# A conditioned transformer layer: own output projection of the last sequence and first MLP weights inside its beats, an fp32 conditioning product, a table of its own for the first sequence

## The chip, the cores and the metric

The kernel runs on one core of one Trainium2 chip. The metric is the device time of one execution in microseconds, as the median of three runs. Below, PE is TensorE, ACT ScalarE, DVE VectorE, POOL GpSimd, and SP the engine that issues the DMA transfers.

## The reference

Everything is float32. There are 8 sequences of 512 tokens of width 512 (`x`) and one conditioning row of width 512 for each.

```python
cond = jax.nn.silu(c) @ wc.T + bc                        # 8 x 3072
sh1, sc1, g1, sh2, sc2, g2 = jnp.split(cond, 6, axis=-1)
h = _ln(x) * (1.0 + sc1) + sh1
x = x + g1 * _gqa_attn(h, wq, wk, wv, wo)                # 16 query heads, 4 key heads, head width 32
h = _ln(x) * (1.0 + sc2) + sh2
x = x + g2 * _mlp(h, w1, b1, w2, b2)                     # width 2048, exact gelu
```

`_gqa_attn` projects q, k and v, takes softmax(q k / sqrt(32)) v by head, and projects with `wo`.

## The kernel before

**Precision.** Large products run on operands split into a high and a low part of a faster float type. ACT copies the high part out of the accumulator bank, DVE subtracts it to get the low part, and PE makes three passes: high x high, high x low, low x high. Values (`values`) and softmax sums (`sums`) run in plain fp32; in them four products of 32 output rows each stand in four column groups of the array.

**The front** (`before` of each engine) is one order written out by hand, `FRONT`, that all engines follow, each doing its own part of a token. `Wc0.1` transposes piece 1 of the conditioning weights c0 (PE) and splits it (ACT `weight_high` L779, DVE `weight_low` L960); `Wk`, `Wq`, `Wv`, `Wo` do so for the projection weights. `Mc0.1` multiplies the piece with silu(c), both halves (`multiply`, L1206). `B0` adds the bias, `C0` turns the part into columns, `S` is silu. `X0` and `X1` are statistics and epsilon of sequences 0 and 1, `N0`, `N1` their norms, `T0` to `T3` the transposes of the normed x with modulation (L692) and split. `K`, `Q0` to `Q3`, `V` are projections; a letter a to d is a quarter, that is one tile of the contraction in three passes. `r0` to `r15` are the row products of group 0 (L1137) with their row maxima (L898), `s0` to `s4` the first of group 1, `t` turns the maxima. SP loads the raw weights and x, and moves K, Q and the maxima into the stacked tiles `k_stack` and `q_stack` (`stack_k`, `stack_q`, `stack_max`).

**A sequence** is 4 groups (one for each key head) of 16 beats. In every beat PE computes one score product (L1150), ACT its exp (L741), and PE one row product for a later group. In a group POOL adds the exps of the four key tiles (L607), PE forms values of two tiles in beat 5 and two in beat 11, and the sums in beat 5; then ACT and DVE invert, refine, divide and split. Between these, PE does the *fill* of the beat: a table gives for each beat the quarters of projections and the transposes. `FILL` serves sequences 0 to 6 (in sequence 0 without the O tokens), `LAST_FILL` sequence 7. `O0` to `O3` are the output projection of the sequence before; `VT` turns V. ACT takes a bank one beat after its token, DVE two or three.

**The last sequence** makes only two of the three adds of a group before the sums, and the sums of two tiles instead (8 products, L1173). Its own output projection, 4 tiles of 12 passes (L1082), comes after its last beat (`after`): groups 0 to 2 of tiles 0 and 1, weights 0 of the MLP turned, tiles 2 and 3, weights 1 turned, then group 3 of all tiles. Group 3 waits for the end of the softmax chain. `gate` (L948) takes each tile.

**The MLP** runs by sequence over 16 slices j: an up product of 12 passes (L1613), gelu and split, a down product of 12 passes into four banks (L1625). In its first sequence the weights of slice j + 1 are loaded through a ring of three, turned (L1379, L1384) and split just ahead. `WEIGHTS_AHEAD` says how many slices are turned before the loop.

The order that all this follows is the order of each engine's own instructions; semaphores join them. An engine that waits holds up everything behind it in its own order.

## Time and profile before

| | |
|---|---|
| Median of 3 runs | 1463.69 us (1463.34 to 1464.05) |
| Profiled execution | 1462.65 us, span 1460.9 us |
| PE busy | 1433.4 us, 98% |
| DVE, ACT, POOL busy | 708.7, 708.2, 569.4 us |
| Mean granted PE clock | 0.995 of full |
| HBM read, written | 55.44, 16.81 MB |

The profiled execution is one run. Its span goes from the first to the last instruction. Times of stages are cut from it: the front ends with the first score at 70.7 us, sequence 0 with the first score of sequence 1 at 146.6, sequence 7 has its last score at 717.3, and the second up product of the MLP starts at 737.8. Busy times of PE include the modelled ends of matmuls, which overlap the next ones; the distance between two starts is what one costs.

### The profile page before, as it was taken

The numbers are of one execution on the slowest core, as the hardware profiler recorded it, in microseconds if no ns is written. First come the engines' busy times: TensorE is split into PE (matmuls) and PEld (weight loads), VectorE is DVE, ScalarE is ACT, GpSimd is POOL, SyncE is SP. The second block draws the span as 40 slices with busy tenths as digits, with TensorE's granted clock in tenths as the row PEclk, the third lists the DMA queues.
The fourth block names the chain that finished last, engine by engine and source line by source line (L and its number), as shares of the span: only waits on it lengthen the run. The fifth ranks groups of instructions, "written<-read, shape, count | busy, mean of one in ns | idle before, by whom it ended". The sixth has DMA issues, their size and how long they took to land.

```text
span 1460.9 us, 19071 instructions
## 1 busy us (share of the span) xinstructions
PE 1433.4 (98%) x7021; PEld 1042.0 (71%) x7021; DVE 708.7 (49%) x1205; ACT 708.2 (48%) x1274; POOL 569.4 (39%) x230
## 2 busy tenths in 40 slices
PE   7899999999999999999999999999999999999998
PEld 5655666656656665665588888888888888888887
DVE  6877777776867787677534321222212122131212
ACT  6376758575666758575644423333233332323321
POOL 2067587676868687675310210121201212012210
PEclk9999999999999999999999999999999999999999
DMA  8232322324232322322352210201102020020100
GB/s 301 67 83 56 107 59 83 104 84 116 78 105 55 106 82 82 112 85 59 124 151 80 72 66 1 93 0 52 41 0 93 0 70 23 0 93 0 65 1 29
DMA packets 68435, 105.15 MB, mean 72 GB/s; under 512 B 10552, under 2 KB 19784, under 8 KB 68368
## 3 DMA queue, kind: packets, MB, share of 16 engines
q1 hardware_dynamic: 68368, 104.27, 23.2%
q8 instruction: 40, 0.66, 0.2%
q14 instruction: 27, 0.22, 0.1%
HBM read 55.44 MB, written 16.81 MB: 49 GB/s over the span
## 4 chain that ended last, share of the span: by engine, by line
PE 90%; DVE 5%; ACT 1%; POOL 1%; issue 1%; DMA 1%; SPq 1%; DVEq 0%; ACTq 0%; POOLq 0%
PE up L1613 24%; PE acc L1625 24%; PE proj_bank L1082 14%; PE key_bank L1150 8%; PE pv_bank L1159 7%; PE row_bank L1137 7%; DVE neg_max L898 3%; PE sum_bank L1173 2%; POOL probs_sum L607 1%; PE turn L1599 1%; PE proj_bank L1092 1%; SPq L486 1%; PE key_bank L1193 0%; ACT probs L741 0%; PE turn L1379 0%
## 5 line engine op out<-in xcount | busy, mean ns | idle before, releaser
L898 DVE TENSOR_REDUCE neg_max<-row_bank 128x1 f32<-128x512 f32 x512 | 337.4, 684 | 141.0 <-PE row_bank L1137 136.7
L741 ACT ACTIVATE probs<-key_bank 128x512 f32<-128x512 f32 x512 | 299.8, 598 | 163.2 <-PE key_bank L1150 159.8
L1613 PE MATMUL up<-h,w_t 128*128 128x512 f32 x1536 | 369.9, 390 | 0.0
L1625 PE MATMUL acc<-w_t,hidden 128*128 128x512 f32 x1536 | 369.6, 390 | 0.0
L1625 PEld LDWEIGHTS acc<-w_t,hidden 128*128 128x128 f32 x1536 | 287.9, 188 | 59.3
L1613 PEld LDWEIGHTS up<-h,w_t 128*128 128x128 f32 x1536 | 286.9, 188 | 58.5
L1544 DVE TENSOR_TENSOR hidden<-up,hidden 128x512 fp32r<-128x512 f32 x128 | 88.5, 692 | 482.6 <-ACT hidden L1495 482.6
L1486 ACT ACTIVATE up<-up,bias_cols 128x512 f32<-128x512 f32 x128 | 84.8, 662 | 421.9 <-PE up L1613 421.9
L607 POOL TENSOR_TENSOR probs_sum<-probs_sum,probs 128x2048 f32<-128x2048 f32 x59 | 271.8, 4607 | 14.4 <-ACT probs L741 7.9
L1150 PE MATMUL key_bank<-q_stack,k_stack 128*128 128x512 f32 x512 | 217.8, 429 | 2.6 <-ACT probs L741 2.5
L1137 PE MATMUL row_bank<-k_stack,q_stack 96*128 96x512 f32 x512 | 204.4, 410 | 4.2 <-DVE neg_max L898 3.6
L1457 POOL TENSOR_TENSOR y<-y,resid 128x512 f32<-128x512 f32 x30 | 37.8, 1293 | 365.1 <-DVE y L1553 365.1
L607 POOL TENSOR_TENSOR probs_sum<-probs 128x2048 f32<-128x2048 f32 x31 | 142.4, 4595 | 90.2 <-ACT probs L741 90.2
L1150 PEld LDWEIGHTS key_bank<-q_stack,k_stack 128*128 128x128 f32 x512 | 96.4, 189 | 83.5 <-issue 49.2
L1137 PEld LDWEIGHTS row_bank<-k_stack,q_stack 96*128 96x128 f32 x512 | 96.7, 189 | 39.8 <-DVE neg_max L898 17.0
L1159 PE MATMUL pv_bank<-probs,v 128*32 128x512 f32 x1024 | 123.1, 598 | 0.0
L1082 PE MATMUL proj_bank<-h,wq_t 128*128 128x512 f32 x384 | 110.4, 401 | 0.0
L1082 PE MATMUL proj_bank<-wo_t,attn 128*128 128x512 f32 x336 | 94.0, 394 | 0.0
L1434 POOL TENSOR_TENSOR rstd<-var_eps,neg_half 128x4 f32<-128x4 f32 x7 | 7.1, 1018 | 213.2 <-DVE var_eps L1530 213.2
L1082 PEld LDWEIGHTS proj_bank<-h,wq_t 128*128 128x128 f32 x384 | 72.3, 190 | 21.0 <-issue 5.9
L1495 ACT ACTIVATE hidden<-up 128x512 fp32r<-128x512 f32 x128 | 76.7, 599 | 11.6
L614 POOL TENSOR_TENSOR resid<-resid,gated 128x512 f32<-128x512 f32 x32 | 40.7, 1286 | 99.0 <-DMA resid<-in_x_dram 69.1
(155 smaller groups left out, 1129.4 us busy)
## 6 DMA issues: line engine op xcount, KB each, us to landing
q_stack<-spare SPq DMA_DIRECT2D x384, 64.0 KB, 2.0
xa<-in_x_dram SPq DMA_DIRECT2D x8, 1024.0 KB, 9.6
resid<-in_x_dram SPq DMA_DIRECT2D x8, 1024.0 KB, 7.0
x_scratch<-resid SPq DMA_DIRECT2D x8, 1024.0 KB, 4.5
xa<-x_scratch SPq DMA_DIRECT2D x8, 1024.0 KB, 5.7
spare<-in_L_cond_w_dram SPq DMA_DIRECT2D x32, 256.0 KB, 3.0
resid<-x_scratch SPq DMA_DIRECT2D x8, 1024.0 KB, 6.6
out_dram<-y SPq DMA_DIRECT2D x7, 1024.0 KB, 4.2
```

The costliest lines, as they stand in the source:

```text
L607: nc.gpsimd.tensor_tensor(probs_sum[:, :, :], first_in[:, :, :], probs[kt][:, :, :], ALU.add).then_inc(added, 1)
L741: nc.scalar.activation(probs[kt][:, r, :], key_bank[r % 2][:, :], ACT.Exp).then_inc(exp_done, 1)
L898: nc.vector.tensor_reduce(out=neg_max[:, g % 2, i:i + 1], in_=row_bank[(g + i) % 2][:, :], op=ALU.max, axis=AX.X, negate=True).then_inc(ro ...
L1082: last = nc.tensor.matmul(bank, lhs(i, kt), rhs(j, kt), start=(kt == 0 and (i, j) == (0, 0)), stop=(kt == KD - 1 and (i, j) == (1, 0)))
L1137: nc.tensor.matmul(row_bank[(g + i) % 2][:, :], q_stack[0:STACK, g, r, qt * P:qt * P + P], k_stack[0:STACK, g, :], start=True, stop=True). ...
L1150: nc.tensor.matmul(key_bank[r % 2][:, :], k_stack[:, g, kt * P:kt * P + P], q_stack[:, g, r, :], start=True, stop=True).then_inc(keys_scor ...
L1159: last = nc.tensor.matmul(pv_bank[HD * r:HD * r + HD, :], v[:, kt, g * HD:g * HD + HD], probs[kt][:, r, :], start=(kt == 0), stop=(kt == T ...
L1486: nc.scalar.activation(up[j % 2][:, :], up[j % 2][:, :], ACT.Gelu, bias=bias_cols[:, j:j + 1]).then_inc(gelu_done, 1)
L1495: nc.scalar.activation(hidden[j % 2][0][:, :], up[j % 2][:, :], ACT.Copy).then_inc(hid_hi, 1)
L1544: nc.vector.tensor_tensor(hidden[j % 2][1][:, :], up[j % 2][:, :], as_f32(hidden[j % 2][0][:, :]), ALU.subtract).then_inc(hid_split, 1)
L1613: last = nc.tensor.matmul(up[j % 2][:, :], w1_t[i][:, kt, j * P:j * P + P], h[k][:, kt, :], start=(kt == 0 and n == 0), stop=(kt == KD - 1 ...
L1625: last = nc.tensor.matmul(acc[tt][:, :], hidden[j % 2][i][:, tt * P:tt * P + P], w2_t[k][:, j, :], start=(j == 0 and n == 0), stop=(j == N ...
```

## The change

1. **Conditioning.** The conditioning weights are no longer split. ACT copies them as fp32 (`copy_weight`) into plain tiles, and PE multiplies two pieces at a time, one into output rows 0 to 7 and one into rows 32 to 39 of a bank; DVE adds both to the bias as before. c0 is loaded in two halves. The loads have a new order, given in `LOADS`, with `wq` ahead of x.
2. **The front's order** is new. `X1` and `N1` leave it; statistics and norms of sequence 1 stand in beats 0 to 11 of sequence 0.
3. **Sequence 0** gets its own fill table, `FIRST_FILL`.
4. **The last sequence** makes all three adds (the third on DVE in the last group, on POOL in the others) and sums of one tile. `U0`, `D0` to `U2`, `D2` turn and split the up and down weights of the first three MLP slices inside its beats, and the loads of these are issued after the maxima of group 2. `L0` to `L3` are quarters a and b (groups 0 and 1) of its own output projection. They use the row banks and the projection banks.
5. **After the last beat**: values, sums, quarter c of the four tiles, the first up product, then quarter d of the four tiles.
6. The MLP weights stand in one tensor `w_t`, by slice; the up banks now lie where the key banks were.

```diff
-WEIGHTS_AHEAD = 2
+WEIGHTS_AHEAD = 3
...
+FIRST_FILL = {
+    (0, 0): ("", "VT Q3a", "", "Q3b"),
+    (0, 1): ("Q3cd", "", "", ""),
+    (0, 2): ("", "", "", ""),
+    (0, 3): ("", "T0", "T1", ""),
+    (1, 0): ("", "", "T2", "T3"),
+    (1, 1): ("", "", "Kab", "Kc"),
+    (1, 2): ("Kd", "Q0ab", "", ""),
+    (1, 3): ("", "Q0c", "", "Q0d"),
+    (2, 0): ("", "", "", "Q1a"),
+    (2, 1): ("", "", "Q1b", ""),
+    (2, 2): ("", "Q1cd", "", "Q2a"),
+    (2, 3): ("Q2b", "", "Q2c", "Q2d"),
+    (3, 0): ("", "Va", "", "Vb"),
+    (3, 1): ("", "", "", ""),
+    (3, 2): ("", "Vcd", "", ""),
+    (3, 3): ("", "", "", ""),
+}
...
-    (0, 0): ("Q3a", "Q3bc", "", "Q3d"),
-    (0, 1): ("", "", "VT", ""),
-    (0, 2): ("", "", "", ""),
-    (0, 3): ("", "", "T0", ""),
-    (1, 0): ("O0a", "O0b", "", "O0c"),
-    (1, 1): ("", "", "O0d", ""),
-    (1, 2): ("", "O1ab", "", ""),
-    (1, 3): ("O1c", "", "", ""),
-    (2, 0): ("", "O1d", "O2a", ""),
-    (2, 1): ("", "", "O2b", ""),
-    (2, 2): ("O2c", "O2d", "", ""),
-    (2, 3): ("", "O3a", "", "O3b"),
-    (3, 0): ("", "O3cd", "", "T1 T2"),
-    (3, 1): ("", "", "", ""),
-    (3, 2): ("T3", "", "", ""),
-    (3, 3): ("", "", "", ""),
+    (0, 0): ("Q3a", "Q3b", "", "Q3cd"),
+    (0, 1): ("", "", "", ""),
+    (0, 2): ("VT", "", "", ""),
+    (0, 3): ("", "T0", "", ""),
+    (1, 0): ("O0ab", "", "", ""),
+    (1, 1): ("", "", "O0c", "O0d"),
+    (1, 2): ("O1a", "", "O1bc", ""),
+    (1, 3): ("O1d", "O2a", "", "O2b"),
+    (2, 0): ("O2c", "O2d", "U0", ""),
+    (2, 1): ("", "", "D0", ""),
+    (2, 2): ("", "T1", "", ""),
+    (2, 3): ("", "O3ab", "", "O3c"),
+    (3, 0): ("O3d", "U1", "T2 L0a", "L0b"),
+    (3, 1): ("D1", "", "", ""),
+    (3, 2): ("U2", "T3", "", "D2"),
+    (3, 3): ("L1a", "L1b", "", "L3ab L2ab"),
...
+FIRST_STATS = (0, 1, 2, 3)
+FIRST_MOMENTS = 4
+FIRST_EPS = 5
+FIRST_SHIFT = 7
+FIRST_NORM = (7, 9, 10, 11)
...
+    table = FIRST_FILL if not has_last else FILL if has_next else LAST_FILL
...
-S Wc0.0 Wc0.1 Wc0.2 Mc0.0 Wc0.3 Wc1.0 Wc1.1 Mc0.1 Mc0.2 Mc0.3 B0 X0 Wk.0 Wc1.2 C0 Mc1.0 Wc1.3 Mc1.1 Wq.0 Wq.3 Mc1.2
-Mc1.3 B1 N0 Wq.1 Wq.2 C1 Wc2.0 Wc2.1 Wv.0 T0 Mc2.0 Wc2.2 Wo.1 T1 Mc2.1 T2 Wc2.3 Mc2.2 Wc3.0 T3 Wo.2 Wo.0 Ka Mc2.3 B2 Kb
-Kc Kd Q0a Q0b Q0c Q0d Wc3.1 Mc3.0 Wc3.2 Wc3.3 Wo.3 Mc3.1 Mc3.2 Mc3.3 B3 r0 r1 Wc4.0 Q1a r2 r3 Wc4.1 Mc4.0 r4 C3 r5 Wc4.2
-Q1b r6 Wc4.3 Q1c r7 r8 Wc5.0 Mc4.1 Mc4.2 Mc4.3 r9 r10 B4 Q1d Va Wc5.1 Mc5.0 r11 r12 Vb r13 Mc5.1 r14 C4 r15 Wc5.2 b1
-Wc5.3 Vc t s0 Vd Mc5.2 X1 Q2a Mc5.3 s1 Q2b Q2c B5 s2 Q2d N1 s3 s4
+Wc0.0 Wc0.1 S Mc0.1 Wc0.2 Wc0.3 Mc0.3 Wc1.0 Wc1.1 Wc1.2 B0 X0 Mc1.1 Wc1.3 Wk.0 Wq.1 Wq.3 Wq.0 Mc1.3 B1 N0 C0 Wq.2 Wc2.0
+C1 Wc2.1 T0 Wo.1 Wc2.2 Wc2.3 T1 Mc2.1 Wo.2 T2 Wv.0 Mc2.3 T3 Wc3.0 Ka Kb Kc B2 Kd Q0a Wc3.1 Wc3.2 Q0b Wo.0 Q0c Q0d Wc3.3
+Wo.3 Mc3.1 Mc3.3 Q1a B3 r0 r1 Wc4.0 Wc4.1 C3 r2 Wc4.2 Q1b r3 r4 Mc4.1 r5 Wc4.3 r6 Wc5.0 r7 Q1c r8 Mc4.3 r9 r10 B4 Q1d Va
+r11 r12 Vb Wc5.1 Wc5.2 C4 Wc5.3 r13 Vc r14 Vd b1 r15 Mc5.1 t s0 Mc5.3 s1 Q2a s2 Q2b B5 s3 Q2c s4 Q2d
 """.split()
 FRONT += [f"s{i}" for i in range(5, 16)]
-RAW, EARLY = 4, 22
+RAW = 4
+LOADS = ('c1', 'q', 'x', 'k', 'c2', 'o', 'v', 'c4', 'c3', 'c5', 'b3', 'b4', 'b1')
...
+EARLY = sum(t[0] == "W" for t in FRONT[:FRONT.index("r0")])
...
+        w_t = sb(st, "w_t", [P, NJ, 4, N], f32r)
...
-            sums = [(g * GROUP + (kt + 1) * R, "sum", kt) for kt in range(1, adds_in(B - 1) + 1)]
+            sums = [(g * GROUP + (kt + 1) * R, "sum", kt) for kt in range(1, TT)]
...
-            return None if tt < 2 else row_bank[tt - 2]
+            return row_bank[tt] if tt < 2 else proj_bank[tt - 2]
...
+            def load_first_part():
+                for i in range(2):
+                    cols = slice(i * D // 2, i * D // 2 + D // 2)
+                    sp.dma_start(raw["c0"][:, :, cols], wc[0:D, cols].rearrange("(o p) i -> p o i", p=P)).then_inc(first_loaded[i], 16)
...
-                sp.dma_start(b1_rows[:, :], b1.rearrange("(j p) -> j p", p=P)).then_inc(b1_loaded, 16)
+                load_first_part()
+                for i in (0, 1, 2, 5):
+                    load_bias(i)
+                for name in LOADS:
+                    if name == "x":
+                        load_x(x, 0)
+                    elif name == "b1":
+                        sp.dma_start(b1_rows[:, :], b1.rearrange("(j p) -> j p", p=P)).then_inc(b1_loaded, 16)
+                    elif name in ("b3", "b4"):
+                        i = int(name[1])
+                        sp.wait_ge(cols_turned, i - 2)
+                        load_bias(i)
+                    elif name[0] == "c":
+                        if name == "c5":
+                            sp.wait_ge(w_turned, w_of("Wc1.3") + 1)
+                        load_part(int(name[1]))
+                    else:
+                        if name == "o":
+                            sp.wait_ge(w_turned, w_of("Wc0.3") + 1)
+                        load_raw(name, {"k": wk, "v": wv, "q": wq, "o": wo}[name])
...
-            def after(b):
+            def load_first_weights(b):
 
                 for g in range(HKV):
                     sp.wait_ge(k_stacked[g], b * STACKED + STACKED)
                     for i in range(2):
                         sp.wait_ge(q_stacked[i][g], queries_stacked(b, 2))
-                load_resid(b)
                 for j in range(RING):
                     load_weights(sp, j)
+
+            def after(b):
+                load_resid(b)
 
...
+            def first_high(name, u):
+                act.wait_ge(proj_ready, u.ready(name))
+                if name[1] != "0":
+                    act.wait_ge(proj_ready, u.ready("O3"))
+                nc.scalar.activation(first_weights(name, 0), proj_bank[u.bank(name)][:, :], ACT.Copy).then_inc(first_hi, 1)
...
-                if g == HKV - 1 and not has_next and 0 < kt <= adds_in(b) and r == R - 1:
+                if g == HKV - 1 and not has_next and kt > 0 and r == R - 1:
...
+            def turn_first(name, u):
+                j, half = int(name[1]), "UD".index(name[0])
+                bank = room(u, name)
+                pe.wait_ge(w_loaded[j], 32)
...
+            def own_part(tt, groups):
+
+                if 0 in groups and tt < 2:
+                    pe.wait_ge(row_taken, row_no(B - 1, HKV - 1, ROWS) + 1)
+                elif 0 in groups:
+                    for who in ("act", "dve"):
+                        pe.wait_ge(proj_taken[who], after_units().base[who])
+                out_part(B - 1, tt, None, groups, after_bank(tt))
+
             def out_part(b, tt, u, groups, bank=None):
 
                 if 0 in groups and bank is None:
                     room(u, f"O{tt}")
-                if tt == 0 or HKV - 1 in groups:
-                    pe.wait_ge(attn_split, b * HKV + (max(groups) + 1))
+                pe.wait_ge(attn_split, b * HKV + (max(groups) + 1))
...
-                pe.wait_ge(added, adds_no(b, g) + adds_in(b))
+                pe.wait_ge(added, adds_no(b, g) + (TT - 1))
                 if not is_first:
                     pe.wait_ge(attn_split, group_no(b, g))
-                summed = [probs_sum] + ([probs[TT - 1]] if adds_in(b) < TT - 1 else [])
-                if len(summed) > 1:
-                    pe.wait_ge(exp_done, exps_no(b, g, TT - 1) + R)
-                for i, tile in enumerate(summed):
-                    for r in range(R):
-                        last = nc.tensor.matmul(sum_bank[HD * r:HD * r + HD, :], ones[:, :], tile[:, r, :],
-                                                start=(i == 0), stop=(i == len(summed) - 1))
+                for r in range(R):
+                    last = nc.tensor.matmul(sum_bank[HD * r:HD * r + HD, :], ones[:, :], probs_sum[:, r, :], start=True, stop=True)
                 last.then_inc(sums_ready, 1)
...
+                n = products.index(w_of("W" + token[1:])) // 2
+                i, half = divmod(n, KD // 2)
+                pe.wait_ge(w_copied, 2 * n + 2)
                 if n == 0:
-                    pe.wait_ge(silu_split, 1)
-                if kt == 0 and i > 0:
+                    pe.wait_ge(silu_taken, 1)
+                if half == 0 and i > 0:
                     pe.wait_ge(part_biased, i)
-                for half in range(2):
-                    last = nc.tensor.matmul(cond_bank[0:SILU, :], silu_both[:, kt, :], wc_t[n % 3][half],
-                                            start=(kt == 0 and half == 0), stop=(kt == KD - 1 and half == 1))
+                for row, kt in ((0, 2 * half), (ODD_ROW, 2 * half + 1)):
+                    last = nc.tensor.matmul(cond_bank[row:row + B, :], silu_cols[:, kt, :], cond_tile(i * KD + kt),
+                                            start=(half == 0), stop=(half == 1))
                 last.then_inc(multiplied, 1)
...
-                    if tt == 2:
-                        pe.wait_ge(row_taken, row_no(b, HKV - 1, ROWS) + 1)
-                    out_part(b, tt, u, range(HKV - 1), after_bank(tt))
-                    if tt % 2 == 1:
-                        turn_weights(pe, tt // 2)
+                    own_part(tt, range(len(own_out(tt)), HKV - 1))
+                pe.wait_ge(proj_taken["dve"], u.base["dve"])
+                first_up(pe)
                 for tt in range(TT):
-                    out_part(b, tt, u, range(HKV - 1, HKV), after_bank(tt))
+                    own_part(tt, range(HKV - 1, HKV))
 
...
+        def up_product(pe, b, j, is_first):
+            if is_first and j < WEIGHTS_AHEAD:
+                pe.wait_ge(*first_split_done(j))
+            elif is_first:
+                pe.wait_ge(w_split, 2 * (j - WEIGHTS_AHEAD) + 2)
+            if not (is_first and j < 2):
+                pe.wait_ge(hid_split, b * NJ + (j - 1))
...
-                    up_product(b, j, is_first)
+                    if not (is_first and j == 0):
+                        up_product(pe, b, j, is_first)
```

## Rows read from the trace of the kernel before

**Rows 1.** The page, section 4: chain that ended last, shares by engine and line.

```profile
PE 90%; DVE 5%; ACT 1%; POOL 1%; issue 1%; DMA 1%; SPq 1%; DVEq 0%; ACTq 0%; POOLq 0%
PE up L1613 24%; PE acc L1625 24%; PE proj_bank L1082 14%; PE key_bank L1150 8%; PE pv_bank L1159 7%; PE row_bank L1137 7%; DVE neg_max L898 3%; PE sum_bank L1173 2%; POOL probs_sum L607 1%; PE turn L1599 1%; PE proj_bank L1092 1%; SPq L486 1%; PE key_bank L1193 0%; ACT probs L741 0%; PE turn L1379 0%
```

**Rows 2.** Busy times by stage: window, length, engines (instructions), PEclk, DMA share, GB/s.

```profile
0.00:44.30 44.30, 33.38 (x188) 25.42 (x189) 27.70 (x49) 26.76 (x47) 10.22 (x15) 0.92 0.73 262
44.30:70.70 26.40, 23.45 (x116) 16.38 (x116) 25.34 (x48) 8.42 (x16) 1.21 (x2) 1.00 0.27 67
70.70:90.20 19.50, 18.75 (x85) 12.13 (x85) 13.63 (x23) 15.13 (x29) 7.82 (x2) 0.91 0.21 53
90.20:109.40 19.20, 18.74 (x95) 10.47 (x94) 13.84 (x23) 12.86 (x25) 15.15 (x4) 1.00 0.37 108
109.40:128.10 18.70, 17.44 (x85) 8.66 (x86) 15.93 (x27) 11.70 (x22) 13.76 (x3) 1.00 0.21 54
128.10:146.60 18.50, 18.50 (x99) 11.16 (x97) 13.93 (x27) 13.76 (x28) 13.74 (x5) 1.00 0.23 56
146.60:229.60 83.00, 82.70 (x434) 51.45 (x433) 62.24 (x106) 55.32 (x107) 61.43 (x19) 1.00 0.29 83
...
702.00:717.40 15.40, 13.49 (x83) 6.32 (x81) 8.22 (x9) 13.10 (x26) 4.55 (x2) 1.00 0.20 76
717.40:737.80 20.40, 20.40 (x118) 14.85 (x118) 9.40 (x14) 7.46 (x12) 4.60 (x4) 1.00 0.58 188
```

**Rows 3.** Groups by line and form: busy us, mean ns; idle before, releaser.

```profile
L898 DVE TENSOR_REDUCE neg_max<-row_bank 128x1 f32<-128x512 f32 x512 | 337.4, 684 | 141.0 <-PE row_bank L1137 136.7
...
L741 ACT ACTIVATE probs<-key_bank 128x512 f32<-128x512 f32 x512 | 299.8, 598 | 163.2 <-PE key_bank L1150 159.8 <-POOL probs_sum L607 1.1
...
L607 POOL TENSOR_TENSOR probs_sum<-probs_sum,probs 128x2048 f32<-128x2048 f32 x59 | 271.8, 4607 | 14.4 <-ACT probs L741 7.9
...
L683 ACT ACTIVATE xa<-xa,shift_col,rstd 128x512 f32<-128x512 f32 x36 | 28.6, 809 | 0.3
...
L960 DVE TENSOR_TENSOR q_stack<-key_bank,q_stack 128x512 fp32r<-128x512 f32 x18 | 12.3, 687 | 6.2 <-ACT q_stack L779 6.0
...
L933 DVE TENSOR_TENSOR probs_sum<-probs 128x2048 f32<-128x2048 f32 x1 | 2.3, 2294 | 0.6 <-ACT probs L741 0.6
```

**Rows 4.** Timeline of PE, two groups of sequence 0: start, us, what.

```profile
90.72 0.86 PE L1082 MATMUL proj_bank<-h,wk_t 128*128 128x512 f32 x3
91.42 0.39 PE L1150 MATMUL key_bank<-q_stack,k_stack 128*128 128x512 f32 x1
91.65 0.40 PE L1137 MATMUL row_bank<-k_stack,q_stack 96*128 96x512 f32 x1
...
95.30 1.92 PE L1159 MATMUL pv_bank<-probs,v 128*32 128x512 f32 x16
97.04 1.04 PE L1173 MATMUL sum_bank<-probs_sum,ones 128*32 128x512 f32 x8
98.01 0.50 PE L1150 MATMUL key_bank<-q_stack,k_stack 128*128 128x512 f32 x1
```

**Rows 5.** Timeline of SP's queue: issuing of Q1's transfers, then of the maxima.

```profile
58.32 7.48 SPq L486 DMA_DIRECT2D q_stack<-spare  x12
65.85 1.22 SPq L493 DMA_DIRECT2D q_stack<-max_row  x2
```

**Rows 6.** Front: statistics of x and first modulation (timeline); landing of x (tile xa).

```profile
15.56 2.45 DVE L873 BATCH_NORM_STATS2 stats<-xa 128x6 f32<-128x512 f32 x4
...
27.55 0.75 ACT L692 ACTIVATE proj_bank<-proj_bank,cond_now 128x512 f32<-128x512 f32 x1
...
DMA to landing us min/median/max: 9.3/9.3/9.3
```

**Rows 7.** Timeline of the tail: last score, last split of the attention output.

```profile
717.34 0.51 PE L1150 MATMUL key_bank<-q_stack,k_stack 128*128 128x512 f32 x1 [0.47 <-ACT probs L741]
...
725.60 0.69 DVE L938 TENSOR_TENSOR wq_t<-sum_bank,wq_t 128x512 fp32r<-128x512 f32 x1 [0.67 <-ACT wq_t L763]
```

290 lines of the change are left out of this document (144 added, 146 removed).

## Prediction

> **What bounds the kernel now.** I read the page's chain of waits first. It is 90% TensorE (PE) [rows 1], so time can only be won where PE stands still or where work is moved into such gaps. Then I cut the span into stages at the first scores of each group and read busy times by stage [rows 2]. PE "busy" there overstates: ends are modelled. So I price PE work by the distance between starts: a row or score product 0.23 us, three passes of a projection ("a quarter") 0.70, two tiles of values 1.74, one set of sums 0.97, including the change into and out of four-column-group work [rows 4]. A transposed tile of four is about 0.4 (mine, between the 0.23 and 0.70 above).
>
> With these prices a group of an ordinary sequence holds 32 x 0.23 + 0.3 (the turned maxima) + 3.48 values + 0.97 sums = 12.1 us, plus its fill. The last group of sequence 0 fills 8 quarters: 17.7 against 18.5 taken [rows 2]. So a full group loses 0.8 us. Emptier groups lose more: group 2 of sequence 0 has 4 quarters, 14.9 of work in 18.7; group 0, with one pair of values and no sums, has 14.4 in 19.5. The last group of the last sequence has no rows: 11.5 in 15.4, with ScalarE (ACT) at 13.1 busy [rows 2]. There the bound is ACT or the wait for it. The front (to 70.7) is another matter: VectorE (DVE) is 25.3 busy of the 26.4 us before the first score [rows 2]. The MLP takes about half of the chain, PE alone [rows 1].
>
> **The change part by part.**
>
> *Front, up to the first row (44.3).* 24 low-part subtractions of wc leave DVE, 0.69 each [rows 3]: 16.5 us. The 48 products at 0.23 [rows 4] (11 us) become 12 pairs of fp32 products. No row has a pair of 8-column fp32 products. The nearest is four 32-column ones side by side, one sum: 0.97 [rows 4]. If two run side by side as those four do, a pair is 0.97 and the total 11.6: about equal. If they run one after the other it is 1.84 and 22.1, the upper bound. A gain is excluded by the same number of streamed columns and passes per product as in the sums. I take 0.97, for the output rows 0 and 32 are two of the same four column groups. But before the first row the front hangs on x: it landed 9.3 us after its issue [rows 6], its statistics ran at 15.56 behind DVE work, and ACT, in order, could not pass the epsilon until they ended; T0 was modulated at 27.55 [rows 6]. The change puts q (1 MB) ahead of x. The stage moved 262 GB/s at a DMA share of 0.73 [rows 2], so 359 at full share, and 1.05 MB takes 2.9 us: x lands near 15 instead of 12, and statistics begin where they do now. What is left is two fewer weight copies by ACT between the norms and T0, one more between T0 and T3 (0.6 each): 0.3 to 0.6 gained. I take **0.3**, bounds -1 and +3. GpSimd's setting of constants (10.2 us busy in all [rows 2]) ends far ahead of the first row and stays hidden; SP's two late bias loads wait for turned columns ahead of the b1 load alone.
>
> *First row to first score (26.4).* Six low-part subtractions and the statistics of x1 (2.45 as for x [rows 6], and with their aggregation about 3.3 by starts) leave DVE here: 4.1 + 3.3 us. DVE then has 16 + 5 row maxima at 0.68 [rows 3] plus two biases of two adds, Q1, Q2 and small copies: about 20. PE holds 21 rows (4.9), 8 transposed weights (3.3), 3 quarters of Q1, V and Q2 (7.7), 4 products (3.9), and turns: 20.5. SP is the third chain: the first score needs the stacked maxima, queued behind the 12 transfers of Q1, 7.5 us, themselves behind Q1's split; the maxima went out at 65.85 [rows 5] and the score came 4.9 later. Q1's split now comes after 11 maxima and one bias, 10 to 11 us from the first row, where it took 14.0; +7.5 +1.2 and 2 for landing gives 21 to 22. The three agree: 22.0 instead of 26.4, **4.4** gained (bounds 2 and 6).
>
> *Sequence 0 (75.9).* It gets its own table and takes statistics and norms of x1 in beats 0 to 11: DVE 3.3, ACT four norms of 0.81 [rows 3] and small steps, 3.7. Work by group becomes 13.4, 18.4, 17.7, 14.9 (it was 14.4, 17.0, 14.9, 17.7). Group 0 is then bound by DVE (16 maxima 11, statistics 3.3, Q3 0.7, a max_low 0.3 = 15.3) and ACT (16 exps 9.6 [rows 3], norms and steps 6.1 = 15.7), and PE waits where they meet: 17.5, less than 19.5, part of which is a clock of 0.91 in that group [rows 2] that I expect gone with the gap before the first score. Groups 1 and 2 are full: 18.4 + 0.8 to 1.2 and 17.7 + 1.1 give 19.5 and 18.8. Group 3: 17.5 at its light fill. Sum 73.3: **2.6** gained, bounds 0 and 5. The wait that ACT takes in beat 5 for moments that DVE ends only after five maxima and four statistics stands ahead of all later exps; this is inside the 17.5. On SP the maxima of group 2 (beat 26) now stand behind K's stacking, whose split comes at beat 26 instead of 21; they are due at beat 32, 7 us later, and 1.9 + 1.2 + 2 fits.
>
> *Sequences 1 to 6.* Same tables, same instructions: 0.
>
> *Last sequence to its last score (73.4).* Sums shrink from 1.84 to 0.97 in three groups, as GpSimd makes the third add. GpSimd then needs 3 x 4.6 [rows 3] and one or two residual adds of 1.3 in groups of 18 to 21, as in the ordinary sequences: hidden; without that cover the sums in beat 5 would wait. Group 0 is as before, group 1 goes from 17.9 to 19.1 of work and loses the stall behind long sums (20.7 instead of 20.8), group 2 from 16.8 to 15.7 (-0.8). Group 3 takes T2, T3, three up and down transposes and 4 quarters; ACT has two more copies (1.2) on a path it bounds: +1.2. Net **-0.3** (bounds +1 and -3.5). SP issues the first six weight loads ahead of the maxima of group 3, some 3.5 us of issuing 16 beats before these are ready: hidden; rings 3 to 5 are loaded before the tail ends.
>
> *Tail, last score to second up product (20.4).* Now: values, sums, 36 passes at 0.23 and four weight transposes ahead of up 0, then the third pair of weights. After: L3 and L2 quarters 2.8, values 1.74, sums 0.97, third quarters 2.8, up 0 2.77 (12 passes), last quarters 2.8 = 13.9 (with up 0 counted in both). Added waits: L3 needs both projection banks, hence the low part of D2, which DVE reaches only after refine, reciprocal, divide, U2 and a 2.29 us add [rows 3]. Queued behind on PE is the whole tail; I get 1.1 us. The third add on DVE ends 3.6 to 4.3 us after the last score, the sums are due at 5.9: hidden. The split of group 3 ended at 726.29 [rows 7], 5.0 us after the sums (717.34 + 0.4 + 1.74 + 1.84); third quarters and up 0 cover 5.6: hidden by 0.6. Down 0 needs four gates and the split of hidden 0 behind them, due within 0.1 us of PE's arrival. So 15.0 for 20.4: **5.4** gained (bounds 3 and 6.5).
>
> *MLP.* Layout only: contiguous operands on both sides, 0.
>
> Sum: 0.3 + 4.4 + 2.6 - 0.3 + 5.4 = 12.4. The profiled run took 1462.65 (span 1460.9, 1.75 around it), so 1450.25; the median stands 1.04 above it: **1451.3 us**.
>
> **A rule of the skill against the row.** Two tiles of values are eight steps of 0.217; the sums, four such steps, take 0.97 to the next score [rows 4]: 0.10 for the change of tiling, and perhaps as much on the way in, so 0.1 to 0.2 us. By the Trainium skill, TensorEngine Tiling (Array Packing), Key Properties, independent tiles run in parallel and changing the mode drains the engine. By that rule the 12 pairs run side by side and pay 12 drains, about 2 us, most of it where PE waits anyway; the trace agrees for four tiles of 32 columns, and shows nothing of two of 8.
>
> **The rivals.**
> *More comes back:* without DVE's 16.5 us and with c0 loaded in halves, the whole front moves up, x is not late, and no stretch falls to the lower clock. For: the 44.3 us to the first row hold 25 us of PE work (26 weights at 0.4, 16 product pairs at 0.47, x 1.6, K and Q0 5.6). Against: x behind q. It adds 3 in the front and 3 in sequence 0: 1445.
> *Less comes back:* fp32 pairs run one after the other. Then PE has 4 x 0.87 more between first row and first score, and some of the other eight show: -5. Or the last group's ACT chain grows by 3. Either gives 1456 to 1457. For: no row shows two tiles of 8.
> *No effect to speak of:* both of these together, or front chains (SP's 12 transfers) that start no earlier: 1461 to 1466.
> *Slower, by the clock:* the front ran at a granted 0.92 to the first row [rows 2], 1.2 GHz for part of it and 2.4 otherwise; it fell after PE's thin start and again around the gap before the first score. The new front starts PE earlier, thinly, and stands waiting for x. If it stays at 1.2 GHz from x's landing on, some 18 of the 25 us double, less the 3 that PE idles there: +15, so 1466 or more, with 1 to 2 beyond for fp32 products. It decides once more than 12.4 + 3 us of PE work on the path runs at half clock. For: a gap at x of 3 to 4 us. Against: the same gap now costs only one such stretch.
> That the change does not do what it says is excluded for the tail, where order is fixed by hand; for the fp32 pairs it is the second rival.
>
> **How the numbers follow.** About 0.2%, or 3 us, is what a measurement of this kernel tells from no change. Chances: forecast (1447 to 1455) 0.54, more 0.17, less 0.17, no effect 0.06, slower by the clock 0.06. Faster by over 0.2% is 0.54 + 0.17 + 0.17 = 0.88; same 0.06, slower 0.06. The range leaves out a tenth at each end, so it takes in most of both neighbours: 1444 to 1459.
>
> **What would show it.** Right: first score near 66; DVE under 21 busy between first row and first score; a fp32 pair at 0.9 to 1.0; sequence 0 at 73 with groups near 17.5, 19.5, 18.8, 17.5; sequences 1 to 6 at 82.8; last score to second up product 15.0 with one wait at L3 for a low part. Wrong: a pair at 1.8, first row later than 45, GpSimd releasing sums in the last sequence, or a granted clock under 0.9 in the front.

## The result

The changed kernel takes 1455.59 us (median of 6 runs, 1454.65 to 1456.29), the kernel before 1463.43 us (6 runs, 1460.87 to 1464.05). The ratio is 0.995, with a 95% interval of 0.9939 to 0.9961: **7.8 us faster**, where the forecast was 1451.3, a gain of 12.4. The time lies inside the range of 1444 to 1459, 0.6 us above the band of the forecast (1447 to 1455). The profiled execution took 1456.24 us, with a span of 1454.2 (before 1462.65 and 1460.9).

The page of after, busy times of the engines and the chain that ended last, by engine. They answer to [rows 1]:

```profile
PE 1424.7 (98%) x6989; PEld 1033.7 (71%) x6989; DVE 696.5 (48%) x1181; ACT 707.4 (49%) x1275; POOL 585.4 (40%) x231
...
PE 88%; DVE 4%; POOL 2%; ACT 2%; SPq 1%; DMA 1%; issue 1%; DVEq 0%; ACTq 0%; POOLq 0%
```

Busy times of after by stage, in the columns of [rows 2]: window, length, PE, PEld, DVE, ACT, POOL, PEclk, DMA share, GB/s. The windows are: to the first row; to the first score; groups 0 to 3 of sequence 0; sequence 1; the last group of the last sequence; from its last score to the second up product.

```profile
0.00:46.46 46.46, 32.82 (x192) 21.31 (x192) 18.80 (x34) 27.69 (x48) 12.56 (x13) 1.00 0.71 250
46.46:68.98 22.52, 22.36 (x112) 14.42 (x113) 17.16 (x30) 6.15 (x12) 0.00 (x0) 1.00 0.28 71
68.98:85.70 16.72, 15.22 (x73) 9.45 (x74) 14.07 (x28) 13.21 (x27) 8.78 (x4) 1.00 0.30 73
85.70:106.60 20.90, 19.76 (x107) 12.00 (x105) 16.11 (x27) 16.26 (x31) 15.28 (x4) 1.00 0.35 99
106.60:125.90 19.30, 19.00 (x98) 11.35 (x98) 16.13 (x28) 12.06 (x23) 13.92 (x4) 1.00 0.21 53
125.90:143.18 17.28, 16.67 (x86) 8.80 (x85) 13.39 (x26) 13.55 (x28) 13.07 (x5) 1.00 0.24 59
143.18:226.51 83.33, 82.64 (x434) 51.38 (x433) 62.13 (x105) 55.10 (x106) 62.02 (x19) 1.00 0.30 82
698.90:716.60 17.70, 15.50 (x95) 8.97 (x95) 10.86 (x12) 14.02 (x27) 7.50 (x3) 1.00 0.28 94
716.60:730.80 14.20, 14.20 (x73) 9.89 (x74) 7.25 (x9) 5.99 (x9) 0.97 (x1) 1.00 0.47 161
```

The rows of the two kernels, subtracted stage by stage:

| stage | before | after | gain | forecast |
|---|---|---|---|---|
| to the first row | 44.31 | 46.46 | -2.15 | 0.3 |
| first row to first score | 26.40 | 22.52 | 3.88 | 4.4 |
| sequence 0 | 75.89 | 74.20 | 1.69 | 2.6 |
| sequences 1 to 6 | 497.41 | 498.60 | -1.19 | 0 |
| last sequence to its last score | 73.33 | 74.80 | -1.47 | -0.3 |
| last score to second up product | 20.45 | 14.24 | 6.21 | 5.4 |
| second to third up product | 6.33 | 6.64 | -0.31 | 0 |
| sum | | | 6.66 | 12.4 |

The sum is the difference of the spans. The third up product to the end takes 716.7 in both kernels and in every kernel below: the layout of the MLP costs nothing. Two lines are spread between executions rather than a cost: sequences 1 to 6 have the same instructions in all kernels, and took between 496.6 and 498.8 in the twelve profiles. Group 2 of the last sequence, with the same instructions, took 18.6 in the profile of after, 17.6 to 17.7 in seven of its ten siblings (the kernels below) and 18.0 to 18.4 in the other three; in after PE waited in it 0.6 us once for GpSimd's adds:

```profile
PE sum_bank L1256 <- POOL probs_sum L662: 0.6, 1, 0.6
```

So a first reading is that the middle and the tail came close to the forecast, and that the front up to the first row went the other way. That was the question for the experiments.

### The profile page after: what moved, and what is told of

It is laid out like the page before. It is cut to its first block, busy times and chain, and to the rows that moved or that the text cites. A ratio compares the mean times of both kernels' runs of the same rounds, so it can differ in the third digit from the quotient of the medians.

```text
span 1454.2 us, 19012 instructions
## 1 busy us (share of the span) xinstructions
PE 1424.7 (98%) x6989; PEld 1033.7 (71%) x6989; DVE 696.5 (48%) x1181; ACT 707.4 (49%) x1275; POOL 585.4 (40%) x231
## 4 chain that ended last, share of the span: by engine, by line
PE 88%; DVE 4%; POOL 2%; ACT 2%; SPq 1%; DMA 1%; issue 1%; DVEq 0%; ACTq 0%; POOLq 0%
PE acc L1712 24%; PE up L1480 24%; PE proj_bank L1153 13%; PE key_bank L1237 7%; PE pv_bank L1246 7%; PE row_bank L1224 7%; DVE neg_max L967 2%; POOL probs_sum L662 2%; PE sum_bank L1256 2%; SPq L532 1%; PE turn L1701 1%; PE turn L1464 1%; DMA gate_now<-gate_scratch 1%; ACT probs L791 1%; PE proj_bank L1163 1%
## 5 line engine op out<-in xcount | busy, mean ns | idle before, releaser
L662 POOL TENSOR_TENSOR probs_sum<-probs_sum,probs 128x2048 f32<-128x2048 f32 x62 | 285.4, 4603 | 14.2 <-ACT probs L791 7.3
L1153 PEld LDWEIGHTS proj_bank<-h,wq_t 128*128 128x128 f32 x384 | 71.6, 189 | 20.7 <-issue 6.7
```

The source lines that it names most:

```text
L662: nc.gpsimd.tensor_tensor(probs_sum[:, :, :], first_in[:, :, :], probs[kt][:, :, :], ALU.add).then_inc(added, 1)
L1153: last = nc.tensor.matmul(bank, lhs(i, kt), rhs(j, kt), start=(kt == 0 and (i, j) == (0, 0)), stop=(kt == KD - 1 and (i, j) == (1, 0)))
```

## The experiments

One table for all, in us of the profiled execution: start of DVE's statistics of x (from which its norm is made), first row, first score, length of sequence 0, last sequence to its last score, from there to the second up product; then the time (with its count of runs where there are several). Each kernel is the changed one with one edit.

| kernel | statistics | first row | first score | seq. 0 | last seq. | to second up | time |
|---|---|---|---|---|---|---|---|
| before | 15.56 | 44.31 | 70.71 | 75.9 | 73.3 | 20.45 | 1463.4 (6) |
| after | 17.78 | 46.46 | 68.98 | 74.2 | 74.8 | 14.24 | 1455.6 (6) |
| e1 silu first | 15.32 | 44.01 | 66.54 | 74.3 | 73.9 | 14.28 | 1453.1 (4) |
| e3 x before q | 18.98 | 47.66 | 70.21 | 74.2 | 73.8 | 14.27 | 1456.3 |
| e6 serial pairs | 19.86 | 49.43 | 74.99 | 74.5 | 74.1 | 14.27 | 1462.0 |
| e9 old order | 15.26 | 44.11 | 68.86 | 74.8 | 73.7 | 14.26 | 1453.8 (4) |
| e10 statistics in front | 18.80 | 47.49 | 73.06 | 77.7 | 73.7 | 14.24 | 1461.8 |
| e2 Q0 whole | 18.14 | 45.47 | 67.99 | 74.2 | 74.4 | 14.27 | 1453.4 |
| e4 U2 earlier | 18.69 | 47.92 | 70.46 | 74.3 | 73.1 | 15.07 | 1456.0 |
| e5 up last | 19.44 | 48.11 | 70.64 | 74.3 | 73.7 | 16.53 | 1458.2 |
| e7 own O after | 18.88 | 47.55 | 70.07 | 74.3 | 73.6 | 18.58 | 1459.8 |
| e8 combined | 13.42 | 40.73 | 63.25 | 74.2 | 74.2 | 14.28 | 1450.2 (5) |

### Who holds up the front

The theory in the prediction was x: the front hangs on its landing. The trace of after showed another chain. Its timeline at the start, PE, ACT and DVE (start, us, what, and in brackets the idle time before it with what ended that):

```profile
4.95 1.94 PE L1279 MATMUL key_bank<-ident,probs 128*128 128x128 f32 x8 [4.95 <-DMA probs<-in_L_cond_wc_dram]
...
7.54 1.28 ACT L823 ACT_TABLE_LOAD   x1
8.83 0.63 ACT L823 ACTIVATE v_full<-v_full 8x512 f32<-8x512 f32 x1
9.48 1.28 ACT L824 ACT_TABLE_LOAD   x1
9.61 0.56 PE L1263 MATMUL pv_bank<-ident,v_full 8*128 8x8 f32 x4 [2.72 <-ACT v_full L823]
...
12.92 1.76 PE L1279 MATMUL row_bank<-ident,probs 128*128 128x128 f32 x8
...
16.45 0.68 DVE L1034 TENSOR_TENSOR gate_now<-sum_bank,gate_now 8x512 f32<-8x512 f32 x1 [16.45 <-PE sum_bank L1292]
...
17.78 2.45 DVE L942 BATCH_NORM_STATS2 stats<-xa 128x6 f32<-128x512 f32 x4
```

`S` now stands behind two weights. ACT copies these, then loads the table of silu, takes silu, and loads the other table back: 7.54 to 10.76, during which PE waits 2.7 us and turns no weight. The third weight is turned at 12.92, the bias B0 comes at 16.45, and the statistics stand behind it in DVE's order, though x had landed at 15.4 (issued at 4.65, 10.7 us to landing). Before, all of this ran ahead of the first weight's landing.

**e1** puts S back to the head.

```diff
-Wc0.0 Wc0.1 S Mc0.1 Wc0.2
+S Wc0.0 Wc0.1 Mc0.1 Wc0.2
```

> The changed kernel with one token moved: silu stands ahead of the first conditioning weights again. Theory A: what made the first row product late (46.46 us instead of 44.31 before) is silu behind two weight copies on ACT. There it costs two table loads and the silu, 7.54 to 10.97, while PE waits 2.7 us; this delays the third weight piece to 12.92, the first bias to 16.45 and, behind that bias on DVE, the statistics of x to 17.78, although x landed at 15.4. With silu first the statistics start at 15.4 to 15.6, T0 is modulated near 26 and the first row comes at 44.0 to 44.7, the first score near 66.8; the whole is 1.5 to 2.4 us faster than the changed kernel. Rival B (what the prediction held): x, behind q in the load order, sets it; then the statistics start no more than 0.3 us earlier and nothing is gained. Rival C: the three transposed weights between the quarters of Q0 set it; then T0 moves but the first row stays within 0.5 us of 46.46.

Measured: 1453.1 us (1451.99 to 1453.78), 0.9931 of before (0.9914 to 0.9947), 2.5 less than after. Its timeline:

```profile
3.03 1.28 ACT L824 ACT_TABLE_LOAD   x1
...
9.02 1.10 PE L1279 MATMUL row_bank<-ident,probs 128*128 128x128 f32 x8
...
11.94 0.68 DVE L1034 TENSOR_TENSOR gate_now<-sum_bank,gate_now 8x512 f32<-8x512 f32 x1 [11.94 <-PE sum_bank L1292]
...
15.32 2.47 DVE L942 BATCH_NORM_STATS2 stats<-xa 128x6 f32<-128x512 f32 x4 [1.99 <-DMA xa<-in_x_dram]
```

The bias comes 4.5 us earlier, the statistics 2.5, the first row 2.45. Only now does x release the statistics: the bracket names its DMA.

The table says more. From the start of the statistics to the first row it is 28.67 to 28.69 us in after, e1, e3, e5, e7 and e10, and 28.75 in before; in e4, whose clock fell in between, it is 29.23. So in these kernels the first row comes early or late by the start of the statistics alone, and this is set by the later of two things: the bias B0, which stands ahead of them on DVE, and the landing of x.

**e3** tests the rival, x, alone.

```diff
-LOADS = ('c1', 'q', 'x', 'k', 'c2', 'o', 'v', 'c4', 'c3', 'c5', 'b3', 'b4', 'b1')
+LOADS = ('c1', 'x', 'q', 'k', 'c2', 'o', 'v', 'c4', 'c3', 'c5', 'b3', 'b4', 'b1')
```

> The changed kernel with x loaded ahead of q. Rival B of the late first row: x sets it, so x landing near 12.7 brings the statistics 2 us or more forward and the first row to 44.5. Theory A (silu's place): the statistics still wait for the first bias on DVE, start at 17.8, and first row (46.5) and time do not move by more than 0.3 us; q, now later, could even cost some tenths.

Measured: x landed 8.8 us after its issue at 4.10, so 2.5 us earlier, and nothing came of it: 1456.3 us. The first row was not at 46.5 as theory A said, but 1.2 us later, as was the bias; more on that below. The timeline of e3 shows the statistics still right behind the bias:

```profile
17.54 1.97 PE L1279 MATMUL key_bank<-ident,probs 128*128 128x128 f32 x8
18.37 0.68 DVE L1036 TENSOR_TENSOR gate_now<-sum_bank,gate_now 8x512 f32<-8x512 f32 x1
18.98 1.26 DVE L942 BATCH_NORM_STATS2 stats<-xa 128x6 f32<-128x512 f32 x2
```

x is refuted as the cause in this order; it is next in line behind silu. The first line shows something else: eight transposes take 1.97 us here at 17.5, and 1.10 in e1 at 9.0. The granted clock of PE rose from 1.2 to 2.4 GHz at 20.0 in e3, at 14.3 in the profile of after, and at 8.7 in e1. (The records of the clock begin with this rise, and the column PEclk of the windows reads 1.00 ahead of it too. The lower level there is read from the transposes: in before, four took 1.05 us at a granted 0.50 and 0.60 at 1.00.)

What a later rise costs is seen where all else in the front is alike: after and e7 have the same front, and their first weights landed at 4.95 and 4.99. The clock rose at 14.3 and 19.7, the statistics started at 17.78 and 18.88, the first row came at 46.46 and 47.55. So 1.1 us are the clock, and e3 with its rise at 20.0 lies where e7 does. Of e1's gain, too, a part is the clock: from the third weight to the bias it took 3.5 us in after and 2.9 in e1, so some 0.6 of the 2.5.

In the trace of before the clock rose at 10.5, but fell again from 17.3 to 24.2 and from 71.9 to 75.4; in that of after it stayed up. In e4, with the same front, it fell from 27.1 to 30.5.

### The fp32 pairs

**e6** sends both products of a pair to the same rows, so that they can't run side by side.

```diff
-                for row, kt in ((0, 2 * half), (ODD_ROW, 2 * half + 1)):
+                for row, kt in ((0, 2 * half), (0, 2 * half + 1)):
...
-                                            start=(half == 0), stop=(half == 1))
+                                            start=(half == 0 and kt == 0), stop=(half == 1 and kt == 3))
...
-                nc.vector.tensor_tensor(cond_rows[i], cond_bank[ODD_ROW:ODD_ROW + B, :], cond_rows[i], ALU.add).then_inc(part_biased, 1)
+                nc.vector.tensor_tensor(cond_rows[i], cond_rows[i], cond_rows[i], ALU.max).then_inc(part_biased, 1)
```

> The changed kernel with both fp32 products of a pair in output rows 0 to 7, one after the other in one accumulation, and the second bias add replaced by one of equal size that changes nothing. It prices the rival of the prediction. Theory: in the changed kernel a pair runs side by side at about 0.87 to 0.95 us; here it takes 1.74 to 1.8. Four pairs stand between first row and first score, eight before. If PE bounds that stretch, first row to first score grows from 22.5 by 3 to 3.5 us and the first row by 1 to 4. If SP's twelve transfers of Q1 or DVE bound it, it grows by less than 1.5 us. The prediction's rival said 5 us in all.

Measured: 1462.0 us. First row to first score took 25.56 where after took 22.52: 3.04 more for four pairs. One pair and the product behind it in the timeline of after, then in that of e6:

```profile
63.88 1.03 PE L1292 MATMUL sum_bank<-cond_w,silu_cols 128*8 128x512 f32 x4
64.84 0.50 PE L1224 MATMUL row_bank<-k_stack,q_stack 96*128 96x512 f32 x1
```

```profile
57.77 1.88 PE L1292 MATMUL sum_bank<-probs,silu_cols 128*8 128x512 f32 x4
59.58 0.73 PE L1224 MATMUL row_bank<-k_stack,q_stack 96*128 96x512 f32 x2
```

From its start to the next start a pair takes 0.96 us side by side and 1.81 one after the other: 0.85 apart, so 3.4 for the four, of which 3.04 show. So PE bounds this stage now. Two tiles of 8 columns at rows 0 and 32 do run side by side, as four of 32 columns do [rows 4]. The rest of the loss lies before the first row, which came 2.97 later than in after.

### The order of the front, and what left it

**e9** keeps the fp32 pairs and S first, but has before's order of tokens (less those that are gone) and of loads.

```diff
-Wc0.0 Wc0.1 S Mc0.1 Wc0.2 Wc0.3 Mc0.3 Wc1.0 Wc1.1 Wc1.2 B0 X0 Mc1.1 Wc1.3 Wk.0 Wq.1 Wq.3 Wq.0 Mc1.3 B1 N0 C0 Wq.2 Wc2.0
+S Wc0.0 Wc0.1 Mc0.1 Wc0.2 Wc0.3 Wc1.0 Wc1.1 Mc0.3 B0 X0 Wk.0 Wc1.2 C0 Wc1.3 Mc1.1 Wq.0 Wq.3
...
-LOADS = ('c1', 'q', 'x', 'k', 'c2', 'o', 'v', 'c4', 'c3', 'c5', 'b3', 'b4', 'b1')
+LOADS = ('c1', 'x', 'k', 'v', 'q', 'c2', 'o', 'c3', 'c4', 'c5', 'b3', 'b4', 'b1')
```

> The changed kernel with the front in the order of the kernel before, less the tokens that no longer exist (half of the products, statistics and norms of sequence 1), and its loads in the old order. It shows fp32 conditioning and the move of sequence 1's statistics without the new order. Theory A: the old order, with silu first, x ahead of q and Q0 in one piece, brings the first row to 42.5 to 44.3, earlier than both; first row to first score is about 22 to 23 as in the changed kernel, since DVE is relieved either way; total 2 to 4 us faster than the changed kernel. Rival D: the new order is what shortens first row to first score; then this stretch is 24 to 26 here and the total is slower than that of the changed kernel.

Measured: 1453.8 us (1453.62 to 1454.33), 0.9935 of before (0.9918 to 0.9951). First row at 44.11, and 24.75 from there to the first score:

```profile
44.11:68.86 24.75, 23.49 (x116) 15.04 (x116) 16.73 (x30) 6.85 (x12) 0.00 (x0) 1.00 0.28 71
```

So of the 3.88 us gained in this stage, 1.65 come with the old order (26.40 to 24.75), by fp32 products and the move of the statistics, which together make DVE lighter, and 2.23 from the new order (to 22.52). Of the two expectations each was half right: the first row came early (theory A), and this stage was long (rival D), yet the total was 1.8 us below after.

Silu's place has to be kept apart from the rest of the order. After has its first score at 68.98, no earlier than e9 (68.86); but e1, the new order with silu first, has it at 66.54, 2.3 us ahead of e9, with first rows at 44.01 and 44.11. So the rest of the new order is a gain, and silu behind two weights gave it back. In the whole time only 0.7 us of this is seen between the medians of e1 and e9, 1.7 between the profiled executions.

**e10** puts statistics and norms of sequence 1 back into the front, with the transposes of sequence 0's table earlier to match.

```diff
-    (0, 2): ("", "", "", ""),
-    (0, 3): ("", "T0", "T1", ""),
-    (1, 0): ("", "", "T2", "T3"),
+    (0, 2): ("T0", "T1", "", ""),
+    (0, 3): ("", "T2", "", "T3"),
+    (1, 0): ("", "", "", ""),
...
-r11 r12 Vb Wc5.1 Wc5.2 C4 Wc5.3 r13 Vc r14 Vd b1 r15 Mc5.1 t s0 Mc5.3 s1 Q2a s2 Q2b B5 s3 Q2c s4 Q2d
+r11 r12 Vb Wc5.1 Wc5.2 C4 Wc5.3 r13 Vc r14 Vd b1 r15 Mc5.1 t s0 Mc5.3 X1 s1 Q2a s2 Q2b B5 s3 Q2c N1 s4 Q2d
...
-                if n in FIRST_STATS and not has_last:
-                    tile_stats(1, FIRST_STATS.index(n))
```

> The changed kernel with statistics and norms of sequence 1 back in the front (behind the last product and behind Q2's third quarter) and its four transposes T0 to T3 in beats 8, 9, 13 and 15 of sequence 0 instead of 13, 14, 18 and 19. It asks where part of the gain of sequence 0 went: group 0 fell from 19.5 to 16.7 us, but group 1 rose from 19.2 to 20.9. Theory: ACT has norms in beats 7 to 11 and then four modulations with copies (5.4 us) in beats 14 to 21, so PE waits for exps at the start of group 1. With the transposes earlier group 1 falls to 18.8 to 19.6, group 0 holds more of PE's work and stays at 16.5 to 17.5, and first row to first score grows from 22.5 by 1 to 2.5 us for the 3.3 us of DVE work. Net 0 to 1 us faster. Rival: group 1 is bound by PE's own fill of eight quarters and two pairs of values, then it stays at 20.5 or more and the net is 1 to 3 us slower.

Measured: 1461.8 us. The windows of e10: first row to first score, groups 0 and 1 of sequence 0; and what PE waited for in the first of them:

```profile
47.49:73.06 25.57, 24.17 (x112) 15.33 (x113) 19.28 (x37) 7.28 (x15) 1.21 (x2) 0.93 0.27 69
73.06:93.90 20.84, 17.99 (x83) 11.48 (x82) 13.62 (x23) 15.19 (x29) 8.19 (x2) 0.92 0.21 51
93.90:114.10 20.20, 19.47 (x100) 11.27 (x98) 14.60 (x24) 13.32 (x26) 14.63 (x4) 1.00 0.36 102
```

```profile
PE row_bank L1213 <- DVE neg_max L961: 1.4, 1, 1.4
```

The stage before the first score is 3.05 longer: PE waits for maxima behind the statistics, and the granted clock is down again, to 0.93 and 0.92 of full. Group 0 takes 20.8 instead of 16.7. Both expectations missed this: the kernel is 6.2 us slower where the theory had a gain and the rival 1 to 3. By stages the move of the statistics is worth 6.5 us in these two profiles, 3.05 here and 3.5 in sequence 0. Not all of it is work: the clock was at half from 49.6 to 53.0 and from 76.9 to 80.3, which by its length costs at most 1.7 us each time (an estimate from these rows). A fall at the start of sequence 0 stands in the profiles of the two kernels that keep these statistics in the front (before and e10) and in none of the other ten. That the waits there bring it about fits, and was not varied by itself.

e10 also answers a question on group 1, which took 20.9 where 19.5 were forecast. I had ACT's norms in mind as its cause. Without norms and with two transposes less it still takes 20.2: both together are 0.6 of it. The rest is its own eight quarters, at 2.5 us above my sum of prices; what in them costs more than the prices was not settled.

**e2** lets the four quarters of Q0 run without weights in between.

```diff
-Kd Q0a Wc3.1 Wc3.2 Q0b Wo.0 Q0c Q0d Wc3.3
+Kd Q0a Q0b Q0c Q0d Wc3.1 Wc3.2 Wo.0 Wc3.3
```

> The changed kernel with the four quarters of Q0 in one piece ahead of the three transposed weights Wc3.1, Wc3.2 and Wo.0. Theory: these three (0.44 us each on PE) stand on the path from T3 by Q0, its split and its transfers to the first row; from the first K product to the end of Q0's split it took 8.48 us in the changed kernel and 7.66 before. Now 7.2 to 7.7, so the first row comes 0.9 to 1.3 us earlier relative to the first K product. The weights that come later are covered by the 3.4 us in which PE waits for Q0's transfers. Rival: the bias of part 3, which stands ahead of the first maximum on DVE, becomes late instead and the distance from first row to first score grows by as much. Compare by distances, for the clock's rise at the start falls at another time in every run (14.3 us in the changed kernel's profile, 8.7 with silu first, 20.0 with x ahead).

Measured: 1453.4 us. From the first product of K to the end of Q0's split 7.13 us instead of 8.48, so 1.35 less, and from first row to first score unchanged at 22.52. Three weights ahead of the last quarters stood on the path; behind them they don't. The time is 2.2 us below after, but 1.5 of the difference lies in sequences 1 to 6, which are the same in both and so spread.

### The tail

In the last group and the tail of after (timeline of PE and DVE from the last group on):

```profile
712.72 0.68 DVE L1023 TENSOR_TENSOR w_t<-proj_bank,w_t 128x512 fp32r<-128x512 f32 x1
713.46 0.66 PE L1171 MATMUL proj_bank<-ident,spare 128*128 128x128 f32 x4 [0.95 <-DVE w_t L1023]
...
716.12 0.68 DVE L1023 TENSOR_TENSOR w_t<-proj_bank,w_t 128x512 fp32r<-128x512 f32 x1
...
716.92 2.95 PE L1153 MATMUL proj_bank<-wo_t,wq_t 128*128 128x512 f32 x12
...
721.55 1.04 PE L1256 MATMUL sum_bank<-probs_sum,ones 128*32 128x512 f32 x8
...
725.39 2.88 PE L1480 MATMUL up<-h,w_t 128*128 128x512 f32 x12
726.78 0.69 DVE L1007 TENSOR_TENSOR wq_t<-sum_bank,wq_t 128x512 fp32r<-128x512 f32 x1 [0.66 <-ACT wq_t L813]
...
730.83 2.88 PE L1480 MATMUL up<-h,w_t 128*128 128x512 f32 x12
```

L3 and L2 (716.92) start with no wait, 0.12 us behind the end of D2's low part (716.12 and 0.68). The wait I had put there came one step earlier, at D2, whose transpose needs U2's bank, and this is low only when DVE has passed its own queue (712.72).

**e4** turns U2 two beats earlier, which takes D2's wait away.

```diff
-    (3, 1): ("D1", "", "", ""),
-    (3, 2): ("U2", "T3", "", "D2"),
+    (3, 1): ("D1", "", "U2", ""),
+    (3, 2): ("", "T3", "", "D2"),
```

> The changed kernel with U2 in beat 54 instead of 56 of the last sequence. In the changed kernel PE stands 1.0 us in beat 59 (3.72 us long, 2.28 in the kernel before) for the low part of U2, which DVE makes only after refine, reciprocal and divide. Theory: with U2 two beats earlier its low part is made ahead of these three, beat 59 falls to 2.3 to 2.7 us, and the last group of the last sequence goes from 17.7 to 16.6 to 17.0; the next wait in the line is that of L3 for the low part of D2, which may take back up to 0.5 of it. Rival: ACT's chain of 16 exps and nine other copies bounds the group, so the stall only moves to the wait for an exp and the group stays at 17.4 or more.

Measured: 1456.0 us, no change. The last group is shorter by 0.7 (16.9 against 17.6 in the siblings), the tail longer by 0.8. The waits of PE around it, first in after (last group), then in e4 (from the last group to after L3):

```profile
PE proj_bank L1171 <- DVE w_t L1023: 1.0, 1, 1.0
```

```profile
PE proj_bank L1153 <- issue: 0.6, 1, 0.6
```

With D2's wait gone the wait at L3 appears. The view names no semaphore, but the timeline of e4 shows what ended it, the low part of D2 on DVE:

```profile
715.90 0.68 DVE L1023 TENSOR_TENSOR w_t<-proj_bank,w_t 128x512 fp32r<-128x512 f32 x1
...
716.68 2.98 PE L1153 MATMUL proj_bank<-wo_t,wq_t 128*128 128x512 f32 x12 [0.64 <-issue]
```

L3 starts 0.10 us behind it, and 18.07 us behind the first score of the group; in after these are 0.12 and 18.01. So one DVE chain, through a 2.28 us add, ends last for both, and it decides.

**e5** puts the first up product behind the last quarters.

```diff
-                pe.wait_ge(proj_taken["dve"], u.base["dve"])
-                first_up(pe)
                 for tt in range(TT):
                     own_part(tt, range(HKV - 1, HKV))
+                pe.wait_ge(proj_taken["dve"], u.base["dve"])
+                first_up(pe)
```

> The changed kernel with the first up product behind the last quarters of its own O instead of ahead of them. Theory: it covers the softmax chain. The last split ended 5.0 us after the sums and only 2.8 us of third quarters are left in between, so PE stands 2.1 to 2.5 us for it and the second up product starts 16.4 to 16.8 us after the last score instead of 14.24. Rival: gates and their residual adds bound the start of the down product in both orders, then the third up product moves by less than 1 us against 20.88.

Measured: 1458.2 us. PE waits in front of the last quarters for the split of group 3, and the second up product starts 16.53 after the last score instead of 14.24, the third 1.9 later than in after:

```profile
PE row_bank L1153 <- DVE wq_t L1007: 2.0, 1, 2.0
```

The up product of 2.8 us covers this wait whole.

**e7** takes the own output projection out of the beats again; all its quarters come after.

```diff
-    (3, 0): ("O3d", "U1", "T2 L0a", "L0b"),
+    (3, 0): ("O3d", "U1", "T2", ""),
...
-    (3, 3): ("L1a", "L1b", "", "L3ab L2ab"),
+    (3, 3): ("", "", "", ""),
```

> The changed kernel with no part of its own O inside the beats: the eight quarters L0 to L3 of groups 0 and 1 go behind the sums. Theory: four of them (2.8 us) filled gaps of a group that ACT bounds, so taking them out shortens the last group by at most 1 us while the tail grows by all eight, less what they now cover: the four quarters of L3 and L2 stood behind the last score and cost PE the same on either side. Last sequence to its last score 73.8 to 74.8, second up product 17.0 after it instead of 14.24: net 2 to 2.8 us slower. Rival: PE bounded the last group, then it shortens by the full 2.8 us and the net is zero.

Measured: 1459.8 us, 4.2 more than after where 2 to 2.8 were expected. Of the eight quarters L0 to L3, four stood in the beats and four behind the last score already. Without them the last sequence is hardly shorter (73.6 against 73.7 to 74.4), so these four were all but free. The tail is 4.3 us longer, more than the 2.8 of four quarters. The windows of e7 before, in and behind the last values, and these values:

```profile
698.00:715.90 17.90, 13.88 (x86) 6.84 (x84) 10.88 (x12) 14.53 (x29) 8.08 (x3) 1.00 0.28 95
715.90:719.40 3.50, 3.50 (x17) 0.78 (x17) 2.85 (x3) 1.00 (x2) 0.00 (x0) 0.51 1.04 378
719.40:737.00 17.60, 17.60 (x84) 13.59 (x80) 5.98 (x10) 4.97 (x7) 3.56 (x3) 1.00 0.17 54
```

```profile
716.52 3.32 PE L1246 MATMUL pv_bank<-probs,v 128*32 128x512 f32 x16
```

The granted clock was 0.51 of full, 1.2 GHz, for 3.5 us right behind a group in which PE was busy for 13.9 of 17.9 us; in after it was busy for 15.5 of 17.7, and its clock stayed up. The values took 3.32 instead of 1.92, so 1.4 us of the difference to 2.8 is the clock. This is one profile, and e4, whose front is that of after, shows that a fall can come in one execution and not in another; what brought this one about is open.

### What the experiments point to

**e8** has S first (e1), Q0 whole (e2) and x ahead of q (e3).

```diff
-Wc0.0 Wc0.1 S Mc0.1 Wc0.2
+S Wc0.0 Wc0.1 Mc0.1 Wc0.2
...
-Kd Q0a Wc3.1 Wc3.2 Q0b Wo.0 Q0c Q0d Wc3.3
+Kd Q0a Q0b Q0c Q0d Wc3.1 Wc3.2 Wo.0 Wc3.3
...
-LOADS = ('c1', 'q', 'x', 'k',
+LOADS = ('c1', 'x', 'q', 'k',
```

> The changed kernel with three of the edits together: silu first, Q0 in one piece, x loaded ahead of q. With silu first the statistics of x waited for its landing (15.3), so now the load order should count: x issued at 4.1 landed 8.8 us later in the run with x ahead, so statistics start behind the first bias at 13.4 to 13.7. The first row then comes at 41.2 to 42.7 us (44.0 with silu first, less 1.35 for Q0, less 0 to 1.5 for x; the conditioning columns or late q may take the place of x). First row to first score 22.5. Median 1450.3 to 1452.3, which would beat both kernels. If q's pieces become the new wait, the first K product does not move against that of the run with silu first (32.2) and the median is 1452 or more.

Measured: **1450.2 us** (1449.47 to 1452.4), 0.9911 of before (0.9897 to 0.9924): faster than both kernels. Its front:

```profile
0.00:40.73 40.73, 31.82 (x192) 20.70 (x192) 18.11 (x33) 26.10 (x47) 12.57 (x13) 1.00 0.82 285
40.73:63.25 22.52, 22.36 (x113) 14.42 (x113) 17.76 (x31) 6.15 (x12) 0.00 (x0) 1.00 0.28 71
```

The order of the loads, worth nothing in e3, now starts the statistics 1.9 us earlier (13.42 against 15.32 in e1): a cause that is second in line shows only once the first is gone.

## Why the prediction was right, and where it was wrong

The gain was forecast at 12.4 and came out at 7.8. The forecast's own band was 1447 to 1455; 1455.59 lies just outside, and inside the range because this takes in most of the rival of less. Neither cause of that rival is what happened: the pairs run side by side, and what the last group took beyond its forecast (17.7 for 16.6) is a wait of 1.0 on DVE, not ACT's chain. So the range held by its width. Two signs of being wrong that the prediction itself named came: the first row was later than 45, and GpSimd released sums in the last sequence once (0.6 us). What held is the mechanism of the three stages that gain.

**To the first row: wrong, and here the forecast was lost.** It said +0.3 and the stage lost 2.15, up to 3.8 in siblings. The step that failed is "before the first row the front hangs on x". I worked out x's landing (15 forecast, 15.4 measured), read that the statistics would begin where they did, and stopped there. I counted the weight copies that ACT loses and gains, but not the token S that moved behind two of them, with its silu and two table loads of 1.28 each. This was to be had from the diff and the trace of before: there both loads lie ahead of the first weight's landing. Every instruction that changes places has to be counted, those of a small token too. e1 shows it at 2.5 us, some 0.6 of it the clock, and e3 shows that x was not the cause. The gain of 0.3 by fewer weight copies was not there either: from statistics to first row it took 28.68 for 28.75. That the three weights between the quarters of Q0 cost 1.35 there (e2) was not in the sum. The Trainium skill, ScalarE: Activation LUTs, What ACT_TABLE_LOAD costs, gives about 1283 ns for a load and 1380 ns more for a drain with each switch. The trace agrees with the first figure and not with the second: load at 7.54, silu at 8.83, next load at 9.48, copy at 10.77, with nothing in between; the copy ahead of the first of these ended at 7.52.

**First row to first score: right in mechanism, short by 0.5** (22.5 for 22.0). The pair costs 0.96 from start to start, as taken (0.97). Three chains were said to agree, PE at 20.5, DVE at 20 and SP at 21 to 22; it is PE that bounds the stage, busy 22.36 of 22.52 us, DVE being busy 17.16, so the sum of PE's work was too small, by what was not settled. That lighter engines carry all of the gain was half right: e9 gives 1.65 to them and 2.2 to the order.

**Serial pairs as a rival: rightly priced where I looked, too cheap in all.** The four pairs cost 3.04 (4 x 0.87 = 3.5 at most), but e6 took 6.4 more than after where the rival had 5 for all; those before the first row count too (49.43 against 46.46). The Trainium skill, TensorEngine Tiling (Array Packing), Key Properties, says that independent tiles run in parallel; the runs now agree for two tiles of 8 columns.

**Sequence 0: right in direction, 1.69 of 2.6.** Groups 16.7, 20.9, 19.3, 17.3 for 17.5, 19.5, 18.8, 17.5. Group 0 is 2.8 us shorter than before; up to 1.7 of that is the clock, which was at half for 3.4 us of it in before (71.9 to 75.4). That it came out 0.8 below the forecast, which had counted on the full clock, was not explained; the sum of prices with 0.8 to 1.2 added was too small for a group with eight quarters and two transposes, and that isn't settled. With the statistics back in the front the stage is 3.5 longer, the fall of the clock included (e10).

**Last sequence: the sum close, by two errors that cancel.** The forecast was 0.3 longer than before, 73.6 to 73.7. The eight siblings with the same tables lie between 73.7 and 74.4, and after at 74.8; which of it is one execution's spread can't be told apart. But group 3 took 17.6 for 16.6: it holds the wait of 1.0 at D2, which is the wait I had put at L3. Against it, group 1 took 20.3 to 20.4 for 20.7, and group 2 mostly 17.6 for 18.2.

**Tail: 6.2 for 5.4, the mechanism right.** 14.24 for 15.0 because L3 doesn't wait. Taken together with group 3, the two are 31.9 in after and 31.6 by the forecast. The DVE chain of D2 is on the path once, in either place (e4). The cover of the last split by the up product holds: the split ended at 727.47 and the last quarters began at 728.11, so 0.64 are to spare for 0.6 forecast, and without the cover PE waits 2.0 (e5).

**Clock: the rival of a slow front didn't come.** Its place was right, though: the clock rises later in the new front (14.3 to 20.2 with silu late, 10.5 before). Its size was about 1 us, not 15 (after and e7). The 0.92 that the prediction read for the front of before holds only the fall from 17.3 to 24.2; the 10.5 us ahead of the first rise are not in it.

## What to carry to other kernels

When a hand-written order is changed, list for each engine every token that changes places, also those that carry no bulk, and look in the trace of before at what covered each of them: a silu with two table loads was free ahead of the first load's landing and cost about 2 us behind it, 2.5 with the clock's later rise. Of two suspects for one wait, change the order of both: the one that stands second shows nothing alone (x, e3) and pays once the first is gone (e8). A stall that is taken away in one place may be the same chain waiting in the next (D2 and L3, e4), so price the chain and not the place.

## What the runs showed of the hardware

- Two fp32 products of 8 columns into rows 0 and 32 run side by side: 0.96 us for a pair from start to next start (after), 1.81 into the same rows (e6).
- A load of ACT's table took 1.28 us, twice for one silu between copies, with no idle time around the two loads (after, 7.54 to 10.77).
- With a PE that stands still between short pieces of work at the start, the clock rose to 2.4 GHz at 8.7 to 20.2 us over the twelve profiles, and at 14.3 to 20.2 in four with the same front (after, e4, e5, e7). Until then eight transposes took 1.94 to 1.97 us, against 1.10 after it.
- In e7 the clock fell to 1.2 GHz for 3.4 us at 716.0, although PE had been busy for 78% of the group before and its longest wait there was 1.0 us. Ahead of the falls named above in before, e4 and e10, too, the longest wait of PE was between 1.2 and 1.8 us.
